# Moving layer-norm statistics, the small product and the running sums of a selective state-space stage to other engines and stages

## The chip, the cores and the metric

The kernel runs on one core of a Trainium2 chip. The metric is the device time of one execution in microseconds (us). The core has a matrix engine (TensorE, PE in the profile; its weight loads are PEld), a vector engine (VectorE, DVE), an engine for activation functions (ScalarE, ACT), a general one (GpSimd, POOL) and one that issues DMAs (SyncE, SP). Each has its own queue of instructions and goes through it in order; they wait for each other by semaphores.

## The reference, cut to what matters

The input x is 32 sequences of 256 tokens of 128 features, with an adjacency matrix of 256x256 for each sequence. Four blocks follow each other, each added to x:

```
x = x + L0_gnn(layernorm(x), adj)      # convolutions, distances, a gated recurrent unit
x = x + L0_ffn(layernorm(x))           # state-space block ("mamba2")
x = x + L1_gnn(layernorm(x), adj)      # d = (sum(adj)+1e-5)**-0.5 ; d*adj*d @ (x @ weight) + bias
x = x + L1_ffn(layernorm(x))           # 8 experts, top 2
```

Of the second block the change touches this:

```
dt    = softplus(layernorm(x) @ W_in[:, 640:644] + dt_bias)     # 4 heads for each token
A     = -exp(A_log)
A_cum = cumsum(dt * A) along the 256 tokens of the sequence (the reference: in chunks of 128)
...     exp(A_cum[l] - A_cum[s]) weighs token s in the output of token l; x*dt enters the sum
out   = Y @ W_out @ W_lin + b_lin
```

## The kernel before, in words

Tokens lie on the 128 partitions: X (x_tokens) holds 64 tiles of 128 tokens by 128 features and stays on the core from stage to stage. A step is 512 tokens (T = 4 tiles, G = 2 sequences), and there are 16 steps. Each stage is a function with a block of its own; between two stages stands a barrier of all engines. There is no planner: the order on each engine is the order in which the code writes it.

The graph stage (gnn_phase) runs a body for each step through every engine, with lags: in VectorE's body number t, part a works on step t-1, b on t-2 and c on t-3, and the last three bodies (16 to 18) only empty the pipeline. Bodies 4 to 15 are a loop with addresses from a register. Part c of a body makes the new state (zd at L455, hT at L458), which TensorE turns back (L566) and VectorE adds to X (L505, semaphore x_updated). Part b ends the body with v (L533) and the argument of n (L537); ScalarE takes its tanh (L430), GpSimd makes x minus tn (L349), and the next body begins with zd. Between zd and the low part of the turned rows (L493) stand the mask product and its split, the normalization of part a (L149), the statistics of the current step (L130, L133), and the sums of the convolution. ScalarE also sums the rows of the adjacency into deg (L438).

The stage of dt (dt_phase) works in 8 pairs of steps. VectorE takes bn_stats (L751) and bn_aggr (L754) of 8 tiles, GpSimd adds epsilon (L708) and takes the power -0.5 (L710), VectorE normalizes (L759), TensorE turns each tile (L798), ScalarE copies the turned rows to XT (L730), and TensorE multiplies each tile with the 4 columns of W_dt (L807): the tile of XT is the stationary operand and 4 columns stream. GpSimd adds the bias b_lin of the block's output to X once a pair is normalized (L716). In the midst VectorE makes dinv from deg (L764 to L768) by one Newton step on ScalarE's exp(-0.5 ln). At the end come, on [128 tokens, 64 tiles x 4 heads], the bias of dt (L775), softplus in three activations (L732 to L736) and a maximum (L778), the product with A (L781), the running sums by two products with a triangle and with ones (L810, L811) and their joining (L783, L785), a transpose (L815), a copy (L742), and two DMAs to DRAM (L692) in the layout of heads by tokens.

The state-space stage (mamba_phase) first reads these sums back, broadcast to all partitions (L866), and runs a software pipeline of 20 bodies. VectorE there adds masks (L952), filters (L968), weighs (L946, L957) and at last updates X (L974) with the output product, four bodies behind the first. GpSimd only takes one power a step (L877). Its weights are loaded by SyncE during the stage of dt (L688). Then follow the dispatch stage and the expert stage.

Of the kernel before, what the change touches and what calls it, by code (L numbers as in the profile page):

```python
# [151 lines left out]
def gnn_phase(nc, x_dram, adjT_dram, adj_dram, w, X, deg, eye):  # L152
# [14 lines left out]
    with ExitStack() as ctx:  # L167
# [26 lines left out]
        rstd = sb("rstd", [P, 2, T])  # L194
        xn = sb("xn", [P, T, P])
# [71 lines left out]
        back_done, x_updated = sem("back_done"), sem("x_updated")  # L267

# [84 lines left out]
        def _(act):  # L353
# [12 lines left out]
            def body(s):  # L366
# [64 lines left out]
                if s.live():  # L431
# [4 lines left out]
                    for j in range(T):  # L436
                        need(act, deg_done, T * s.t + j - 1)
                        act.activation(summed[:, j % 2], adj[:, s.p, j], ACT.Copy, accum_out=deg[:, bass.ds(s.t * T + j, 1)]).then_inc(deg_done, 1)  # L438
# [3 lines left out]
        def _(dve):  # L442
            def body(s):
# [84 lines left out]
                if b.live():  # L528

                    dve.wait_ge(tr_ready, b.t + 1)  # L530
                    dve.wait_ge(gh_ready, b.t + 1)
                    need(dve, u_ready, b.t)
                    dve.scalar_tensor_tensor(out=v[:], in0=tr[:], scalar=1.0, in1=gh[:], op0=ALU.add, op1=ALU.mult).then_inc(rg_ready, 1)  # L533
                    dve.wait_ge(rg_ready, b.t + 1)
                    dve.wait_ge(n_done, b.t + 1)
                    need(dve, tn_ready, b.t)
                    dve.tensor_tensor(n_arg[:], v[:], p_n[:], ALU.add).then_inc(u_ready, 1)  # L537
            run_steps(dve, body, 3)
# [92 lines left out]
def mamba_weights(nc, ctx, w):  # L631
# [7 lines left out]
        "never": ([P, P], w["never"]),  # L639
    }  # L640
# [3 lines left out]
def dt_phase(nc, w, X, XT, table, deg, dinv, next_weights, cum_dram, eye):  # L644
# [3 lines left out]
    PAIR = 2 * T  # L648
    PAIRS = NT // PAIR
    COLS = NT * HEADS  # L650
    with ExitStack() as ctx:
        ph = Phase(nc, ctx, "t_")
        sb, sem = ph.sb, ph.sem
        w_dt = sb("w_dt", [P, HEADS])
        b_lin = sb("b_lin", [P, P])
        dt_bias, A_log, A_neg = (sb(s, [P, HEADS]) for s in ("dt_bias", "A_log", "A_neg"))
        upper, ones = sb("upper", [P, P]), sb("ones", [P, P])
        minus_half = sb("minus_half", [P, PAIR])
        eps = sb("eps", [P, 1])
        stats, mv = sb("stats", [P, 2, PAIR, 6]), sb("mv", [P, 2, PAIR, 2])  # L660
        veps, rstd = sb("veps", [P, 2, PAIR]), sb("rstd", [P, 2, PAIR])
        xn = sb("xn", [P, 2, PAIR, P])
        flat = [P, NT, HEADS]
        u, absu, e, l, dt, dA = (sb(s, flat) for s in ("u", "absu", "e", "l", "dt", "dA"))
        cum, total = sb("cum", flat), sb("total", flat)
        turned = sb("turned", [P, 2, P])
        logs, rough, vr, vrr = (sb(s, [P, NT]) for s in ("logs", "rough", "vr", "vrr"))
        p_xT = [ph.psum(f"p_xT{p}", [P, 2, S]) for p in range(2)]
        p_dt = ph.psum("p_dt", flat)
        p_cum, p_total = ph.psum("p_cum", flat), ph.psum("p_total", flat)  # L670
        p_turned = ph.psum("p_turned", [P, 2, P])
        names = ("loaded next_loaded consts stats_done mv_done veps_done rstd_done xn_ready xT_done XT_ready biased dt_done A_ready "
                 "u_ready e_ready dt_ready dA_ready cum_done cum_ready total_ready turned_done turned_ready table_ready written logs_done rough_done chain")
# [3 lines left out]
        def live(k):  # L677
            return 0 <= k < PAIRS

        @block.sync  # L680
        def _(sp):
            sp.dma_start(b_lin[:], spread(w["b_lin"])).then_inc(q["loaded"], 16)
            sp.dma_start(w_dt[:], w["W_dt"]).then_inc(q["loaded"], 16)
            sp.dma_start(dt_bias[:], spread(w["dt_bias"])).then_inc(q["loaded"], 16)
# [1020 lines left out]
```

## Time and profile before

| | us |
|---|---|
| median of 3 runs | 1245.38 (1243.94 to 1248.22) |
| the profiled execution, own time | 1249.54 |
| its span, first to last instruction | 1247.8 |
| graph stage | 0 to 386.8 |
| stage of dt | 386.8 to 445.5 |
| state-space stage | 445.5 to 766.5 |
| dispatch and expert stages | 766.5 to 1247.8 |

TensorE is busy for 84% of the span, VectorE for 68%, ScalarE for 57%, GpSimd for 32%. Busy time alone does not say what bounds a stage: TensorE's matmuls are pipelined, and its granted clock changes between two levels, 1.0 (2.4 GHz) and 0.5 (1.2 GHz). The mean granted clock over the span is 0.874.

### The profile page before, as it was taken

The page shows a single profiled execution, that of the slowest core. Times are in us where ns is not written, and L with a number is a line of the kernel's source. Part 1 is how long each engine was busy: PE and PEld are TensorE (multiplying, and loading weights), DVE is VectorE, ACT ScalarE, POOL GpSimd, SP SyncE. Part 2 cuts the span into 40 slices and gives each one's busy share as a digit, 9 for nine tenths or more (in the row PEclk, how much of TensorE's full clock was granted, in tenths as well). Part 3 has the DMA queues.
Part 4 walks back from the last instruction along what each step waited for, and adds up shares of the span by engine and source line. Part 5 has one row for each costly group of instructions (what it writes and reads, how often), then busy time and mean ns, then how long its engine had stood idle before and what let it go on. Part 6 is the DMA issues. An engine that isn't in the chain of part 4 may idle for free. (4 is left out here: it accounts for less than half of the span.)

```text
span 1247.8 us, 23207 instructions
## 1 busy us (share of the span) xinstructions
PE 1053.5 (84%) x6746; PEld 925.6 (74%) x6746; DVE 846.9 (68%) x2117; ACT 712.4 (57%) x1560; POOL 400.6 (32%) x413
## 2 busy tenths in 40 slices
PE   2999999999995946899999975567609999899998
PEld 2988889898884924566666665566509999899997
DVE  5576767667667636999999964799854555445554
ACT  4466564655652238888888853666504555455554
POOL 4232232322314600001000001457662444524444
PEclk9999999999996567788788876788658999999999
DMA  4121212112100022123212302735234544333331
GB/s 157 60 69 44 85 42 82 44 44 82 34 1 24 1 72 62 40 68 68 64 47 60 68 1 83 233 112 160 82 128 122 150 127 126 95 96 96 99 95 56
DMA packets 82778, 99.14 MB, mean 79 GB/s; under 512 B 9483, under 2 KB 68626, under 8 KB 82554
## 3 DMA queue, kind: packets, MB, share of 16 engines
q1 hardware_dynamic: 72490, 74.31, 22.0%
q0 software_dynamic: 8752, 21.25, 4.9%
q10 hardware_dynamic: 1440, 2.40, 0.6%
q8 instruction: 48, 0.79, 0.3%
q14 instruction: 48, 0.39, 0.1%
HBM read 72.30 MB, written 27.02 MB: 80 GB/s over the span
## 5 line engine op out<-in xcount | busy, mean ns | idle before, releaser
L1616 PE MATMUL e_p_y<-w,e_gT 128*128 (+1 forms) x852 | 118.2, 275 | 0.0
L1563 DVE TENSOR_TENSOR e_g<-e_sl,e_p_h 128x342 f32<-128x342 f32 x142 | 72.6, 511 | 63.5 <-ACT e_sl L1541 55.5
L877 POOL TENSOR_TENSOR m_rs<-m_ms,m_minus_half 128x4 f32<-128x4 f32 x16 | 18.6, 1164 | 300.5 <-ACT m_ms L910 300.5
L1616 PEld LDWEIGHTS e_p_y<-w,e_gT 128*128 128x128 f32 (+1 forms) x852 | 106.1, 191 | 0.4 <-issue 0.4
L1545 ACT ACTIVATE e_gT<-e_p_gx 128x384 f32<-128x384 f32 x142 | 69.6, 490 | 63.9 <-PE e_p_gx L1606 63.9
L87 PE MATMUL e_p_h<-w_hi,e_xT_hi 128*128 x284 | 104.5, 368 | 1.5 <-DVE e_g L1563 0.8
L1541 ACT ACTIVATE e_sl<-e_p_h 128x342 f32<-128x342 f32 x142 | 64.8, 457 | 69.7 <-PE e_p_h L89 69.5
L1567 DVE TENSOR_TENSOR e_xT_lo<-e_p_gx,e_xT_hi 128x128 fp32r<-128x128 f32 x142 | 41.4, 292 | 86.2 <-ACT e_xT_hi L1549 85.9
L1527 POOL DMA_INDIRECT sorted_scratch<-e_xg x71 | 69.0, 972 | 91.2 <-DVE e_xg L1573 89.6
L1525 POOL DMA_INDIRECT out<-e_xg x71 | 68.9, 970 | 85.9 <-DVE e_xg L1573 79.9
L968 DVE SCALAR_TENSOR_TENSOR m_c<-m_p_x,m_vecs,m_c 128x506 f32<-128x506 f32 (+2 forms) x144 | 95.5, 735 | 0.0
L89 PE MATMUL e_p_h<-w_hi,e_xT_lo 128*128 x284 | 92.1, 324 | 0.0
L88 PE MATMUL e_p_h<-w_lo,e_xT_hi 128*128 x284 | 92.0, 324 | 0.0
L1230 POOL DMA_INDIRECT sorted_scratch<-rows,c_dest x64 | 62.8, 982 | 30.5 <-issue 17.4
L1606 PE MATMUL e_p_gx<-eye,e_g 128*128 128x128 f32 (+1 forms) x426 | 69.6, 272 | 0.0
L1602 PE MATMUL e_p_gx<-eye,e_xg 128*128 128x128 f32 x142 | 39.8, 280 | 30.8 <-DMA e_xg<-sorted_scratch 30.0
L991 PE MATMUL m_p_x<-xT_all,m_w_in 128*128 128x512 f32 x96 | 52.1, 684 | 14.2 <-DVE m_c L968 13.4
L1039 PE MATMUL m_p_zY<-m_W,m_xdt 128*64 128x256 f32 x256 | 61.7, 560 | 2.6 <-DVE m_W L946 2.6
L918 ACT ACTIVATE m_dec<-m_cum,table 128x256 f32<-128x256 f32 x128 | 63.3, 495 | 0.2
L87 PEld LDWEIGHTS e_p_h<-w_hi,e_xT_hi 128*128 128x128 f32 x284 | 55.1, 194 | 2.8 <-issue 2.6
L88 PEld LDWEIGHTS e_p_h<-w_lo,e_xT_hi 128*128 128x128 f32 x284 | 55.2, 194 | 0.0
L89 PEld LDWEIGHTS e_p_h<-w_hi,e_xT_lo 128*128 128x128 f32 x284 | 54.8, 193 | 0.0
(357 smaller groups left out, 3356.3 us busy)
## 6 DMA issues: line engine op xcount, KB each, us to landing
e_xg<-sorted_scratch SPq DMA_DIRECT2D x142, 130.0 KB, 2.1
m_cum<-cum_scratch SPq DMA_DIRECT2D x16, 1024.0 KB
g_adjT<-in_adjT SPq DMA_DIRECT2D x16, 512.0 KB, 4.0
g_adj<-in_adj SPq DMA_DIRECT2D x16, 512.0 KB
c_adjT<-in_adjT SPq DMA_DIRECT2D x16, 512.0 KB, 6.5
x_tokens<-in_x SPq DMA_DIRECT2D x16, 256.0 KB, 5.0
sorted_scratch<-nothing SPq DMA_DIRECT2D x2, 1040.0 KB, 10.1
sorted_scratch<-nothing SPq DMA_DIRECT2D x12, 130.0 KB, 2.6
```

The source lines that it names most:

```text
L87: pe.matmul(out, lhsT.hi, rhs.hi, start=start, stop=False)
L88: pe.matmul(out, lhsT.hi, rhs.lo, start=False, stop=False)
L89: return pe.matmul(out, lhsT.lo, rhs.hi, start=False, stop=stop)
L918: act.activation(dec[:, g, h, lo:hi], rows[b], ACT.Exp, bias=table[:, d * T + 2 * g + b, NEG_CUM, h:h + 1]).then_inc(q["dec_ready"], 1)
L968: dve.scalar_tensor_tensor(out=out, in0=x, scalar=vecs[:, k * TAPS + tap:k * TAPS + tap + 1], in1=out, op0=ALU.mult, op1=ALU.add).then_inc ...
L1525: sent = pool.indirect_dma_start(out_dram, home, xg[:, b, RES:RES + P], None, bounds_check=NT * P - 1, oob_is_err=False)
L1527: sent = pool.indirect_dma_start(sorted_dram[1], home, xg[:, b], None, bounds_check=ROWS - 1, oob_is_err=False)
L1541: act.activation(sl[:, i % 2], p_h1[i % 2][:, 0:HP], ACT.Silu).then_inc(q["sl_ready"], 1)
L1545: act.activation(gT[:, c % D3], p_gx[i % 2][:, 0:len(CH)], ACT.Copy).then_inc(q["gT_ready"], 1)
L1563: dve.tensor_tensor(g[:, i % D3], sl[:, i % 2], p_h3[i % 2][:, 0:HP], ALU.mult).then_inc(q["g_ready"], 1)
L1606: last = pe.transpose(p_gx[i % 2][0:r, k, :], g[:, c % D3, h0:h0 + r], eye[:])
L1616: last = pe.matmul(p_y[d % 2][:, 0:P], gT[0:r, d % D3, k], w2k[:, bass.ts(e, P)], start=k == 0, stop=k == len(CH) - 1)
```

## The change

The change does five things.

1. In the graph stage, VectorE takes the statistics of the updated X (part c of a body): four bn_stats between v and n's argument, four bn_aggr and one copy behind it. Mean and variance go to rows 1 and 2 of a tile `norm` whose row 0 is the old deg.
2. In the stage of dt both roots, of deg and of the variance, are taken at once for all 64 tiles (128 columns): ln and exp on ScalarE, three operations on VectorE. GpSimd's power and the statistics leave the stage, and the 64 normalizations run in a row.
3. The product changes roles: slices of a weight tile that is zero but for W_dt's 4 columns are the stationary operand, 256 columns of XT (a sequence) stream, and 32 such products add up in one bank. Row 4j+h of the result is head h of sequence j. The bias of dt and A are then one number for each row.
4. The running sums are one scan of VectorE along 256 tokens and go to DRAM in one DMA. Two pairs of transposes and four copies of ScalarE bring dt and minus the sums back to the table with tokens on partitions.
5. GpSimd adds b_lin to X in the state-space stage, two adds of 256 columns for each step, behind the power of the step before.

```diff
 # graph stage, VectorE, end of a body
+                    if c.live():
+                        dve.wait_ge(x_updated, c.t + 1)
+                        need(dve, next_norm, c.t)
                     dve.scalar_tensor_tensor(out=v[:], in0=tr[:], ...).then_inc(rg_ready, 1)
+                if c.live():
...
+                    for j in range(T):
+                        dve.bn_stats(next_stats[:, j, :], X[:, c.t * T + j, :]).then_inc(next_stats_done, 1)
+                if b.live():
+                    if c.live():
+                        dve.wait_ge(next_stats_done, T * (c.t + 1))
                     dve.wait_ge(rg_ready, b.t + 1)
...
                     dve.tensor_tensor(n_arg[:], v[:], p_n[:], ALU.add).then_inc(u_ready, 1)
+                if c.live():
...
+                    for j in range(T):
+                        dve.bn_aggr(next_mv[:, j, :], next_stats[:, j, :]).then_inc(next_mv_done, 1)
+                    dve.wait_ge(next_mv_done, T * (c.t + 1))
+                    dve.tensor_copy(norm[:, 1:3, bass.ds(c.t * T, T)], next_mv[:].rearrange("p t k -> p k t")).then_inc(next_norm, 1)
 # stage of dt, SyncE
+            sp.dma_start(per_row[:], w["dt_rows"]).then_inc(q["w_in"], 16)
+            sp.wait_ge(q["cleared"], 1)
+            sp.dma_start(w_dt[:, SEQ_ROWS:P], w["W_dt"]).then_inc(q["w_in"], 16)
...
+            sp.wait_ge(q["cum_ready"], 1)
+            sp.dma_start(cum_dram.rearrange("h (j l) -> j h l", l=N), cum[:]).then_inc(q["written"], 16)
 # stage of dt, GpSimd
+            pool.memset(w_dt[:], 0.0).then_inc(q["cleared"], 1)
 # stage of dt, ScalarE
+            act.activation(logs[:], norm[:, 0:3:2], ACT.Ln, bias=eps[:, 0:1]).then_inc(q["logs_done"], 1)
+            act.activation(rough[:], logs[:], ACT.Exp, scale=-0.5).then_inc(q["rough_done"], 1)
...
+            act.activation(absu[:], p_dt[:], ACT.Abs, bias=per_row[:, 0:1]).then_inc(q["abs_ready"], 1)
+            act.activation(e[:], absu[:], ACT.Exp, scale=-1.0).then_inc(q["e_ready"], 1)
+            act.activation(l[:], e[:], ACT.Ln, bias=1.0).then_inc(q["l_ready"], 1)
+            for k, scale in ((DT, 1.0), (NEG_CUM, -1.0)):
+                act.wait_ge(q["turned_done"], k + 1)
+                for c in range(2):
+                    act.activation(pieces[:, k, c], p_turned[k][:, c]..., ACT.Copy, scale=scale).then_inc(q["table_ready"], 1)
 # stage of dt, VectorE
+            dve.scalar_tensor_tensor(out=vr[:], in0=norm[:, 0:3:2], scalar=EPS, in1=rough[:], ...)   # and two more -> inv
+            for s in range(STEPS):
+                need(dve, q["xT_done"], s - 2)
+                for j in range(T):
+                    t = s * T + j
+                    dve.tensor_scalar(xn[:, s % 3, j, :], X[:, t, :], norm[:, 1, t:t + 1], inv[:, 1, t:t + 1], ALU.subtract, ALU.mult)
+            dve.tensor_scalar(u[:], p_dt[:], per_row[:, 0:1], 0.0, ALU.add, ALU.max)
+            dve.tensor_tensor(dt[:], u[:], l[:], ALU.add)
+            dve.tensor_scalar(dA[:], dt[:], A_pos[:, 0:1], -1.0, ALU.mult, ALU.mult)
+            dve.tensor_tensor_scan(out=cum[:], data0=ones[:], data1=dA[:], initial=0.0, op0=ALU.mult, op1=ALU.add)
 # stage of dt, TensorE: 4 transposes of step s, then the product of step s-1
+                    for g in range(G):
+                        j = b * G + g
+                        last = pe.matmul(p_dt[:], w_dt[:, SEQ_ROWS - HEADS * j:SEQ_ROWS - HEADS * j + P], XT[:, j * N:(j + 1) * N], start=j == 0, stop=j == BS - 1)
 # state-space stage, GpSimd and VectorE
             for s in range(STEPS):
+                for half in range(2):
+                    xt = X[:, s * T + 2 * half:s * T + 2 * half + 2, :]
+                    pool.tensor_tensor(xt, xt, bb, ALU.add).then_inc(q["biased"], 1)
...
                     dve.wait_ge(q["rs_ready"], o + 1)
+                    dve.wait_ge(q["biased"], 2 * (o + 1))
```

The dispatch stage reads row 0 of `inv` in place of dinv, and b_lin is loaded with the weights of the state-space stage.

## Rows read from the trace of the kernel before

**Rows 1.** By stage: stretch, us, busy of PE PEld DVE ACT POOL, clock, DMA.
```profile
0.00:386.80 386.80, 355.76 (x2352) 317.17 (x2352) 256.69 (x519) 214.90 (x441) 113.31 (x131) 0.98 0.20 60
386.80:445.50 58.70, 42.88 (x198) 40.89 (x199) 41.34 (x202) 14.06 (x27) 34.27 (x28) 0.50 0.05 15
445.50:766.50 321.00, 266.10 (x1444) 193.33 (x1444) 262.10 (x336) 237.37 (x434) 18.78 (x19) 0.80 0.23 53
```

**Rows 2.** Timeline of VectorE, one step of the graph stage; start, duration, idle before.
```profile
215.78 0.87 DVE L130 BATCH_NORM_STATS2 g_stats<-x_tokens 128x6 f32 x4
216.56 0.37 DVE L133 BATCH_NORM_AGGREGATE g_mv<-g_stats 128x2 f32<-128x6 f32 x4
...
219.99 0.69 DVE L493 TENSOR_TENSOR g_xs_lo<-g_p_xT,g_xs_hi 128x512 fp32r<-128x512 f32 x1 [0.28 <-ACT g_xf L379]
...
228.62 0.69 DVE L533 SCALAR_TENSOR_TENSOR g_v<-g_tr,g_gh 128x512 f32<-128x512 f32 x1 [1.41 <-ACT g_tr L424]
229.35 0.69 DVE L537 TENSOR_TENSOR g_n_arg<-g_v,g_p_n 128x512 f32<-128x512 f32 x1
232.20 0.69 DVE L455 SCALAR_TENSOR_TENSOR g_zd<-g_tz,g_xd 128x512 f32<-128x512 f32 x1 [2.17 <-POOL g_xd L349]
```

**Rows 3.** Groups of the graph stage, 85 to 350 us; busy, mean ns, idle before.
```profile
L493 DVE TENSOR_TENSOR g_xs_lo<-g_p_xT,g_xs_hi 128x512 fp32r<-128x512 f32 x12 | 8.3, 692 | 4.5 <-ACT g_xf L379 4.5
...
L87 PE MATMUL g_p_nmp<-g_xs_hi,g_w_lr_hi 128*64 128x512 f32 x12 | 5.0, 416 | 1.7 <-DVE g_xs_lo L493 1.4
```

**Rows 4.** Timeline of the start of the stage of dt.
```profile
386.77 1.28 ACT L720 ACT_TABLE_LOAD   x1 [5.90 <-PEq L101]
...
388.44 0.26 ACT L724 ACTIVATE t_rough<-t_logs 128x64 f32<-128x64 f32 x1
...
391.20 2.14 DVE L759 TENSOR_SCALAR t_xn<-x_tokens,t_mv,t_rstd 128x128 f32<-128x128 f32 x8
...
392.37 2.14 PE L798 MATMUL t_p_xT<-eye,t_xn 128*128 128x128 f32 x8 [7.55 <-DVE t_xn L759]
```

**Rows 5.** Groups of the stage of dt, 391 to 435.1 us.
```profile
L807 PEld LDWEIGHTS t_p_dt<-t_w_dt,xT_all 128*128 128x128 f32 x128 | 29.1, 333 | 0.1
...
L759 DVE TENSOR_SCALAR t_xn<-x_tokens,t_mv,t_rstd 128x128 f32<-128x128 f32 x64 | 20.0, 382 | 0.3 <-POOL t_rstd L710 0.2
L716 POOL TENSOR_TENSOR x_tokens<-x_tokens,t_b_lin 128x1024 f32<-128x1024 f32 x8 | 18.8, 2353 | 2.3 <-DVE t_xn L759 2.3
```

**Rows 6.** Timeline of the stage of dt in its steady part.
```profile
404.40 1.83 PEld L807 LDWEIGHTS t_p_dt<-t_w_dt,xT_all 128*128 128x128 f32 x8
...
405.97 0.90 PEld L798 LDWEIGHTS t_p_xT<-eye,t_xn 128*128 128x128 f32 x4
```

**Rows 7.** Timeline of the end of the stage of dt.
```profile
435.06 0.42 DVE L775 TENSOR_TENSOR t_u<-t_p_dt,t_dt_bias 128x256 f32<-128x256 f32 x1 [8.67 <-PE t_p_dt L807]
...
441.81 1.25 SPq L692 DMA_DIRECT2D cum_scratch<-t_turned  x2
```

**Rows 8.** Busy time and granted clock (third number from the end) of short stretches.
```profile
447.50:451.70 4.20, 4.20 (x5) 1.84 (x6) 0.00 (x0) 1.17 (x2) 0.00 (x0) 0.50 0.68 136
451.70:455.10 3.40, 2.43 (x6) 0.76 (x4) 0.15 (x1) 2.09 (x3) 0.00 (x0) 1.00 0.89 278
...
810.10:813.50 3.40, 3.40 (x25) 3.22 (x24) 1.34 (x4) 2.71 (x9) 3.40 (x1) 1.00 0.55 154
```

**Rows 9.** Timeline of TensorE in the dispatch stage, ahead of 810.1.
```profile
806.00 3.62 PE L1425 MATMUL c_p_agg<-c_adjT,c_xs 128*128 128x256 f32 x8
809.41 0.95 PE L1431 MATMUL c_p_xT<-eye,rows 128*128 128x128 f32 x4
```

**Rows 10.** Groups of later stages; for L1319 durations, ns min/median/max.
```profile
L974 DVE SCALAR_TENSOR_TENSOR x_tokens<-m_p_o,m_rs,x_tokens 128x128 f32<-128x128 f32 x64 | 17.8, 339 | 11.0 <-POOL m_rs L877 11.0
...
L1360 DVE TENSOR_TENSOR_SCAN c_upto<-c_restart,c_hot 128x144 f32<-128x144 f32 x8 | 3.7, 461 | 0.3
...
L1319 DVE SCALAR_TENSOR_TENSOR c_vr<-c_mv,c_rough x19: 129/158/4800, 769.2 to 895.5; 128x8 f32<-128x8 f32 x19
```

More of the change, by code:

```diff
@@ L672, in dt_phase @@
-        names = ("loaded next_loaded consts stats_done mv_done veps_done rstd_done xn_ready xT_done XT_ready biased dt_done A_ready "
-                 "u_ready e_ready dt_ready dA_ready cum_done cum_ready total_ready turned_done turned_ready table_ready written logs_done rough_done chain")
+        w_dt = sb("w_dt", [P, SEQ_ROWS + P])
+        per_row = sb("per_row", [P, 2])
+        A_pos = sb("A_pos", [P, 1])
+        eps = sb("eps", [P, 1])
+        ones = sb("ones", [P, N])
+        both = [P, 2, NT]
@@ L781, in _ @@
[L781 to L787 removed]
+            dve.wait_ge(q["A_ready"], 1)
@@ L810, in _ @@
-            pe.matmul(p_cum[:], upper[:], dA[:], start=True, stop=True).then_inc(q["cum_done"], 1)
-            pe.matmul(p_total[:], ones[:], dA[:], start=True, stop=True).then_inc(q["cum_done"], 1)
-            pe.wait_ge(q["cum_ready"], 2)
-            for c in range(2):
-                half = cum[:, c * (NT // 2):(c + 1) * (NT // 2)].rearrange("p t h -> p (t h)")
-                last = pe.transpose(p_turned[:, c], half, eye[:])
-            last.then_inc(q["turned_done"], 1)
+                    for g in range(G):
+                        j = b * G + g
+                        last = pe.matmul(p_dt[:], w_dt[:, SEQ_ROWS - HEADS * j:SEQ_ROWS - HEADS * j + P], XT[:, j * N:(j + 1) * N], start=j == 0, stop=j == BS - 1)
@@ L819, in mamba_phase @@
+            last.then_inc(q["dt_done"], 1)
+            for k, (src, ready) in enumerate(((dt, "dt_ready"), (cum, "cum_ready"))):
+                pe.wait_ge(q[ready], 1)
+                for c in range(2):
+                    last = pe.transpose(p_turned[k][:, c], src[:, c * P:(c + 1) * P], eye[:])
+                last.then_inc(q["turned_done"], 1)
 def mamba_phase(nc, weights, X, XT, table, cum_dram, eye):
@@ L829, in mamba_phase @@
         sb, sem = ph.sb, ph.sem
-        w_in, w_outT, w_lin, vecs, D, never = (weights[name][0] for name in ("w_in", "w_outT", "w_lin", "vecs", "D", "never"))
+        w_in, w_outT, w_lin, vecs, D, never, b_lin = (weights[name][0] for name in ("w_in", "w_outT", "w_lin", "vecs", "D", "never", "b_lin"))
         w_out = sb("w_out", [P, 2, P])
```

197 lines of the change are left out of this document (66 added, 131 removed).

## The prediction

> **What bounds the kernel now.** I read the stages first, by stretches [rows 1]: the graph stage up to 386.8 us, the stage of dt from there to 445.5 (58.7 us), the state-space stage to 766.5. The engines separate what bounds each. In the graph stage TensorE is busy for 355.8 of 386.8 us at a granted clock of 0.98, and what can lengthen it is whatever makes TensorE wait. In the stage of dt TensorE's matmul row is busy for 42.9 of 58.7 us at 0.50, the lower of its levels (1.2 GHz), with VectorE at 41.3 beside it. Next the groups of that stage [rows 5] and its order of time [rows 6]: once it runs, TensorE alternates 8 weight loads of the product (1.83 us, so 0.23 each, two passes for each tile of tokens) with 4 transposes (0.90), 2.46 us from one step to the next. The product streams 4 columns and pays 128 rows of weights for them. The rest of the stage is a start (392.4 before TensorE begins) and a chain of single operations at the end, from 435.06 to 445.5 [rows 1, 7].
>
> The graph stage I read by one step of VectorE [rows 2], because the change puts work between two of its lines. A step is 22 us. After n's argument (229.35) VectorE idles 2.17 us until GpSimd has x minus tn, then runs with hardly a gap to the low part of the transposed rows (219.99), before which it idles 0.28. Over 12 steps that idle time is 4.5 us, 0.37 a step, and TensorE's first product on these rows waited 1.4 us in all for that very line [rows 3]. So TensorE's order and the loop through VectorE are nearly equally long.
>
> **The change part by part.** All against the profiled execution (span 1247.8, own time 1249.54), which lies 4.2 us above the median 1245.38; differences are carried over unscaled.
>
> (1) *Statistics in the graph stage.* Per step VectorE gets 4 bn_stats between v and n_arg, and 4 bn_aggr and a small copy behind n_arg. The same forms take 0.87 and 0.37 there [rows 2]; the copy of 8 elements is not shown in that stage, I bound it by 0.1 and 0.4 and take 0.2. The aggregation and copy (0.6) lie in the 2.17 idle behind n_arg. The statistics do not lie beside anything: n_arg starts 0.04 behind v's end now, in the changed kernel 0.91 later. Queued behind n_arg are ScalarE's tanh, GpSimd's subtraction, VectorE's zd, and then VectorE's unbroken row of work down to the low part at 219.99. Its idle 0.37 absorbs a part; 0.91-0.37 = 0.54 us reach TensorE. It is a loop from step to step, so it is paid each time: the statistics stand in bodies 3 to 15, the low part behind each in bodies 4 to 16, 13 times: +7.0 us. Ends: 0 (TensorE has slack I don't see), and 13x1.28 = 16.6 (aggregation on the path too and no idle time). In the last two bodies VectorE has no statistics and normalization of its own left, which covers it; only behind the last update of X nothing covers: 0.87+0.37+0.2 = +1.4 us ahead of the barrier. Sum of (1): +8.4.
>
> (2) *Start of the stage of dt.* Gone: statistics and GpSimd's power; now in series: table load 1.28 and two activations [rows 4], 128 wide instead of 64 (the second took 0.26; I take 0.4 and 0.3), three VectorE operations of 128 columns at 0.29 (between the 0.26 of that row and the 0.42 of the 256 wide one in rows 7), then 4 normalizations of 0.27 (8 in 2.14). With the gaps TensorE starts some 4.2 us into the stage instead of 5.6 (392.37). GpSimd now clears the weight tile before SyncE may load the 4 columns of W_dt, and ScalarE's 16 copies and TensorE's first product stand behind that load. It is issued some 0.5 us in, and the first product wants it at about 5.5; the nearest row, the write of the sums, has 3.7 us from issue to the next stage with two issues in it [rows 1, 7], so it lands in time. If that cover is gone, its lateness (up to 1 us) is paid once.
>
> (3) *The product.* 32 products of 256 columns, each two passes, in place of 64x2 weight-bound ones: 4 passes a step. Nearest row: 128x256 f32 passes, 8 in 3.62 us at the low level, so 0.43 each (the last one's latency off), 0.21 by half at the high one [rows 9]. The loads hide under 256 columns there. With 4 transposes (0.90 low [rows 6], 0.45 high) a step is 4x0.43+0.90 = 2.62 us low and 1.31 high. At the low level nothing is gained over 2.46. The level decides. In the trace it rose behind products streamed back to back in the next stage, low at 447.5 and high at 451.7 [rows 8]; at 810.1 it was high after 256-column products at the low level and 4 transposes [rows 8, 9]. It stayed low through 43 us of 4-column products and transposes. The new mixture has long products in each step with transposes between, nearer to 806-810 than to the old stage. I take: low for the first two steps (5.2 us), then high: 14x1.31 = 18.3. VectorE, no longer with statistics, needs 64x0.27 = 17.3 us, under TensorE's 23.5; at the old stage's mean of 0.38 it would be 24.3, about TensorE's time. That mean has GpSimd's 8 adds of 2.35 us beside it [rows 5], and those leave. Product until the last result: 5.2+18.3+0.3 = 23.8, ends 21.0 (high at once) and 42.3 (never).
>
> (4) *End of the stage.* Three activations of 256 (0.45 with their gaps), sum 0.45, times A 0.4, scan. The scan's nearest row is 144 wide in 0.46 [rows 10]; by length 0.8, ends 0.42 (the elementwise row of rows 7) and 0.85. Then one write to DRAM instead of two; from its issue at 441.81 to the next stage are 3.7 us [rows 1, 7], of which 1.25 were two issues; one goes: 3.1. Transposes and table copies (about 1.3 us behind the scan) lie beside the write. 1.35+0.45+0.4+0.8+3.1 = 6.1 us against 10.4.
>
> Stage: 4.2+23.8+6.1 = 34.1 against 58.7: -24.6.
>
> (5) *Bias in the next stage.* 32 adds of 256, by 2.35 for 1024 some 0.6 us, 18.8 in all, on GpSimd, which is busy for 18.8 of 321 us there [rows 1]. Two stand behind each power; VectorE at that time works on taps and on forms with one operand in PSUM. In the stage behind, where GpSimd adds rows too, those forms never stretched (339 ns mean over 64 [rows 10] for the update of X), while an 8-wide one with both inputs in SBUF went from a median of 158 ns to 4800 at most [rows 10]. I take 0; ends 0 and +18.8 (every add blocks VectorE). It gives nothing back, since it is added work. The new wait on the bias stands four steps behind the adds. The stage's running sums still come by the same DMA behind the same barrier.
>
> **Sum**: +8.4-24.6+0 = -16.2: 1249.5 becomes 1233.3, the median 1245.4 becomes 1229.2.
>
> **Rivals.** (A) the forecast, 1229: chance 0.50. (B) The statistics in the graph stage find cover, as the busy TensorE there suggests (0.98 clock, almost no gaps): no +7.0, so 1222. For it: most of TensorE's products waited for nothing; against: rows 3. Chance 0.17. (C) TensorE's clock stays at 1.2 GHz, because the transposes between the products break the activity. Stage 4.2+42.3+6.1 = 52.6, -6.1; with +8.4 that is +2.3: 1247.7, and up to 1253 when the aggregation (13x0.37) stands on the path as well. It decides from where the stage is longer than 50.3 us (58.7-8.4), there it is slower than before. For: the old stage never rose with transposes in it; against: 810.1. Chance 0.20. The Trainium skill, "TensorE: Matmul & The Clock Gate", section "PE-mode transpose", says that transposes don't count as busy time for the clock in the same way; by that rule this rival gains, and no row here separates them. (D) The adds in the state-space stage hold up VectorE, which is busy 262 of 321 us: half of the 18.8 gives 1239. Against: 339 ns. Chance 0.08. Small rest 0.05, spread over the ends.
>
> **Numbers.** 0.3% (3.7 us) is what can be told from no change. Faster by more: A, B, D and a little of the rest, 0.75. Within: C mostly, 0.13. Slower by more: C's upper part, 0.12. Range: B's 1222 less 2 for a clock that rises at once, to C's 1247: 1220 to 1247.
>
> **What would show it.** In the profile after: bn_stats between v and n_arg, the idle time before the low part gone, and TensorE's first product on it waiting about 0.5 us in each step (B: no wait); granted clock of the new stage mostly 1.00 (C: 0.50) and a step of 1.3 us (C: 2.6); from the last product to the next stage 6 us; two-input SBUF lines of the state-space stage unstretched (D: stretched). The prediction is wrong if the stage of dt takes over 45 us or the graph stage grows by less than 3 or more than 14 us.

## The result and the profile after

| us | before | changed |
|---|---|---|
| median, same chip | 1244.8 (1243.66 to 1248.22, 5 runs) | 1223.17 (1221.25 to 1223.77, 5 runs) |
| ratio to before | | 0.9818, interval 0.9801 to 0.9834 |
| profiled execution, own time | 1249.54 | 1222.53 |
| graph stage | 386.8 | 389.2 |
| stage of dt | 58.7 | 34.4 |
| state-space stage | 321.3 | 315.2 |
| dispatch, expert stage | 166.2, 314.8 | 166.4, 315.4 |

The changed kernel is 21.6 us faster by the medians; 16.2 were forecast. Its 1223.2 lies nearer to rival B (1222) than to the forecast (1229); what that is worth is said behind the experiments. Stages below are cut at the table load that opens each, which puts the state-space stage of the kernel before at 321.3 us.

Stretches of the changed kernel (busy of PE, PEld, DVE, ACT, POOL; granted clock third from the end). The first three rows answer to [rows 1], the last two cut the stage of dt where the clock rose:

```profile
0.00:389.20 389.20, 354.90 (x2352) 316.05 (x2352) 272.37 (x663) 215.16 (x440) 113.53 (x130) 0.99 0.20 59
389.20:423.60 34.40, 25.24 (x132) 20.77 (x132) 20.32 (x71) 13.95 (x27) 0.59 (x3) 0.80 0.09 24
423.60:738.80 315.20, 262.00 (x1444) 190.66 (x1444) 262.03 (x336) 236.96 (x434) 40.44 (x51) 0.81 0.24 54
389.20:398.80 9.60, 5.27 (x18) 4.28 (x19) 6.53 (x25) 3.83 (x7) 0.59 (x3) 0.50 0.27 70
398.80:419.30 20.50, 18.59 (x111) 15.91 (x110) 12.71 (x45) 9.23 (x17) 0.00 (x0) 1.00 0.01 1
```

VectorE's busy time moved with the statistics: +15.7 us in the graph stage, -21.0 in the stage of dt. The stage lost 24.3 us: its clock went from 0.50 throughout to 1.00 for 20.5 us of it, and its two ends got shorter.

The steady part of the stage of dt, changed kernel, timeline (start, duration); it answers to [rows 6]:

```profile
400.65 0.60 PE L772 MATMUL t_p_xT<-eye,t_xn 128*128 128x128 f32 x4
400.98 0.73 PEld L780 LDWEIGHTS t_p_dt<-xT_all,t_w_dt 128*128 128x128 f32 x4
401.08 1.03 PE L780 MATMUL t_p_dt<-xT_all,t_w_dt 128*128 128x256 f32 x4
401.29 1.12 DVE L751 TENSOR_SCALAR t_xn<-x_tokens,norm,inv 128x128 f32<-128x128 f32 x4 [0.19 <-PE t_p_xT L772]
401.95 0.60 PE L772 MATMUL t_p_xT<-eye,t_xn 128*128 128x128 f32 x4
```

From one group of four transposes to the next are 1.30 us. VectorE waits for TensorE (0.19), not the reverse. Its end, answering to [rows 7]:

```profile
415.41 1.98 PE L780 MATMUL t_p_dt<-xT_all,t_w_dt 128*128 128x256 f32 x8
...
417.43 0.47 ACT L726 ACTIVATE t_absu<-t_p_dt,t_per_row 128x256 f32<-128x256 f32 x1 [1.22 <-PE t_p_dt L780]
...
418.90 0.42 DVE L756 TENSOR_TENSOR t_dt<-t_u,t_l 128x256 f32<-128x256 f32 x1 [0.48 <-ACT t_l L730]
419.36 0.35 DVE L759 TENSOR_SCALAR t_dA<-t_dt,t_A_pos 128x256 f32<-128x256 f32 x1
...
419.75 0.69 DVE L762 TENSOR_TENSOR_SCAN t_cum<-t_ones,t_dA 128x256 f32<-128x256 f32 x1
...
420.47 0.61 SPq L703 DMA_DIRECT2D cum_scratch<-t_cum  x1
```

The second pair of turned pieces is copied by 421.7, and the next stage begins at 423.6: the write sets the end, as forecast.

VectorE in one step of the graph stage, changed kernel, answering to [rows 2] (figures in brackets: idle time):

```profile
207.07 0.69 DVE L538 SCALAR_TENSOR_TENSOR g_v<-g_tr,g_gh 128x512 f32<-128x512 f32 x1 [1.41 <-ACT g_tr L426]
207.68 0.87 DVE L544 BATCH_NORM_STATS2 g_next_stats<-x_tokens 128x6 f32 x4
208.58 0.69 DVE L551 TENSOR_TENSOR g_n_arg<-g_v,g_p_n 128x512 f32<-128x512 f32 x1
209.18 0.38 DVE L556 BATCH_NORM_AGGREGATE g_next_mv<-g_next_stats 128x2 f32<-128x6 f32 x4
209.71 0.17 DVE L558 COPY norm<-g_next_mv 128x8 f32 x1
211.42 0.69 DVE L457 SCALAR_TENSOR_TENSOR g_zd<-g_tz,g_xd 128x512 f32<-128x512 f32 x1 [1.54 <-POOL g_xd L351]
...
219.66 0.48 DVE L488 SCALAR_TENSOR_TENSOR g_v<-g_odd,g_scales,g_xf 128x256 f32<-128x256 f32 x1
220.05 0.69 DVE L491 TENSOR_TENSOR g_nm_lo<-g_p_nmp,g_nm_hi 128x512 fp32r<-128x512 f32 x1
220.65 0.68 DVE L495 TENSOR_TENSOR g_xs_lo<-g_p_xT,g_xs_hi 128x512 fp32r<-128x512 f32 x1
```

The idle time ahead of the low part (L495) is gone. How little that cost is read below.

### The profile page after: what moved, and what is told of

Its sections match the earlier page's. It is cut to its first block and busy times, and to the rows that moved or that the text cites. A ratio compares the mean times of both kernels' runs of the same rounds, so it can differ in the third digit from the quotient of the medians.

```text
span 1220.7 us, 23165 instructions
## 1 busy us (share of the span) xinstructions
PE 1028.3 (84%) x6680; PEld 898.8 (74%) x6680; DVE 842.0 (69%) x2130; ACT 712.4 (58%) x1561; POOL 388.8 (32%) x421
## 5 line engine op out<-in xcount | busy, mean ns | idle before, releaser
L942 DVE SCALAR_TENSOR_TENSOR m_c<-m_p_x,m_vecs,m_c 128x506 f32<-128x506 f32 (+2 forms) x144 | 95.6, 740 | 0.0
```

What stands on the lines that cost most here:

```text
L942: dve.scalar_tensor_tensor(out=out, in0=x, scalar=vecs[:, k * TAPS + tap:k * TAPS + tap + 1], in1=out, op0=ALU.mult, op1=ALU.add).then_inc ...
```

## The experiments

The runs lie on several chips. On two of them (one had the first set of four, the other the statistics taken twice) the dispatch stage takes 177 to 180 us and not 166, and before itself has a median of 1259, so ratios and the other stages are compared. The first set: again, statistics back, statistics behind, warm start.

**Again.** The changed kernel, unchanged, on another chip, to compare the others of its set with.

> The changed kernel again, as a control for its neighbours and for how much a stage's length differs from one execution to another. Theory 1 (the state-space stage is 5.8 us shorter for a reason in the change): that stage takes 315 to 316 us again, total 1223. Rival (it was that execution's fall of the clock's rises and of the reads of the running sums): that stage comes out anywhere from 315 to 321 us.

Ratio 0.9819 (0.9786 to 0.9853); graph 389.8, dt 34.8, state-space 314.8 us. It reproduces, stage by stage.

**Statistics back in the stage of dt**, in a row ahead of the roots; the graph stage as before.

```diff
-                if c.live(): ... dve.bn_stats(next_stats[:, j, :], X[...]) ... dve.bn_aggr(...) ... dve.tensor_copy(norm[:, 1:3, ...])
+            for t in range(NT):
+                dve.bn_stats(stats[:, t, :], X[:, t, :]).then_inc(q["stats_done"], 1)
+            for t in range(NT):
+                dve.wait_ge(q["stats_done"], t + 1)
+                dve.bn_aggr(mv[:, t, :], stats[:, t, :]).then_inc(q["mv_done"], 1)
```

> Undoes part 1 alone: 64 bn_stats (0.20 us each, back to back) and 64 bn_aggr (0.08) and one copy stand at the start of the stage of dt on VectorE, the graph stage has none. Theory 1 (in the graph stage the statistics cost next to nothing, 0.11 us a step and 1.4 at the end): the graph stage is 2.4 us shorter, 386.8 again, the stage of dt longer by 13.2+5.0+0.2-1 (the table load runs beside) = 17.5, total 1223.2-2.4+17.5 = 1238. Rival (they cost 0.54 us a step there, and something else in that stage was quicker in the profiled execution): the graph stage is 8.4 us shorter, total 1232.

Ratio 0.9916 (0.9889 to 0.9943). Graph 386.9, so the moved statistics cost that stage 3.0 us (389.82 against 386.85); dt 50.5, so they would cost 15.7 there (17.5 expected). Of their 16.8 us little more than the table load beside them is covered in a stage of dt built like this one: its groups there (busy, mean ns, idle before) are

```profile
L722 DVE BATCH_NORM_STATS2 t_stats<-x_tokens 128x6 f32<-128x128 f32 x64 | 12.5, 288 | 1.3 <-PEq L101 1.3
L725 DVE BATCH_NORM_AGGREGATE t_mv<-t_stats 128x2 f32<-128x6 f32 x64 | 4.3, 175 | 0.0
```

**Statistics behind n's argument**, so that tanh and all behind it start no later.

```diff
-                    for j in range(T):
-                        dve.bn_stats(next_stats[:, j, :], ...)          # between v and n_arg
                     dve.tensor_tensor(n_arg[:], v[:], p_n[:], ALU.add).then_inc(u_ready, 1)
                 if c.live():
+                    for j in range(T):
+                        dve.bn_stats(next_stats[:, j, :], ...)
                     for j in range(T):
                         dve.bn_aggr(next_mv[:, j, :], ...)
```

> Moves the four bn_stats of the graph stage from before n's argument to behind it, ahead of the aggregation; the aggregations then wait one by one. Theory 1 (VectorE's idle 1.54 us before zd takes them in, and what they cost before n's argument is the 0.11 us a step): 13x0.11 = 1.4 us faster than the changed kernel, 1221.8; the graph stage ends 1.4 us sooner. Rival A (the step's length comes from TensorE alone and the 0.11 is the waits and addresses): no difference. Rival B (0.87+0.37+0.17 plus the gaps do not fit before x minus tn arrives: 2.17 us before): up to 0.3 us a step slower, 1227.

Ratio 0.9812 (0.9784 to 0.9841), graph 387.4: 0.5 us above the kernel without statistics there. One step of it, timeline:

```profile
228.70 0.69 DVE L543 TENSOR_TENSOR g_n_arg<-g_v,g_p_n 128x512 f32<-128x512 f32 x1
229.30 0.86 DVE L549 BATCH_NORM_STATS2 g_next_stats<-x_tokens 128x6 f32 x4
230.09 0.37 DVE L552 BATCH_NORM_AGGREGATE g_next_mv<-g_next_stats 128x2 f32<-128x6 f32 x4
230.60 0.94 DVE L554 COPY norm<-g_next_mv 128x8 f32 x1
231.55 0.69 DVE L457 SCALAR_TENSOR_TENSOR g_zd<-g_tz,g_xd 128x512 f32<-128x512 f32 x1
```

n's argument starts 0.73 us behind v again, and the whole set fits in the time that VectorE waits for GpSimd. The gain of 2.4 us in that stage (389.8 to 387.4, where 1.4 was expected) is seen in the profile; the medians of the total, 1237.4 and 1237.5, show no gain.

**Statistics taken twice**, the second set between v and n's argument too, into a spare tile.

```diff
+                    for j in range(T):
+                        dve.bn_stats(spare[:, j, :], X[:, c.t * T + j, :])
                     for j in range(T):
                         dve.bn_stats(next_stats[:, j, :], X[:, c.t * T + j, :]).then_inc(next_stats_done, 1)
```

> The changed kernel with each step's four statistics between v and n's argument taken twice; the second set goes to a tile that nobody reads (about +0.8 us of VectorE per step, 13 steps). The first set cost the graph stage about 1.5 us in its loop where 7.0 was forecast. Theory A (the loop had 0.7 us of slack per step, and the first set used it up): now every further us is paid, 13 x 0.8 = +10 us, graph stage 398 to 401 instead of 389.5, VectorE's zd starts every 22.8 to 22.9 us instead of 22.11, no idle time ahead of the low part of the turned rows, total about 1233. Theory R (TensorE has a large reserve there and statistics at this place cost little whatever their number): graph stage +1 to +3 us (390 to 392.5), total about 1225.

Graph 401.1, +11.3 on the 389.8 of the changed kernel's second profile (+11.9 on the first): 13 x 0.8 = 10.4, and 0.8 more behind the last update of X, which the expectation left out. zd starts every 22.92 us (103.73 to 332.96 in 10 steps) against 22.11 and, in the kernel before, 22.00. What TensorE's first product on the low part waited for it, 12 steps of the changed kernel, then of this one (groups; last column the wait):

```profile
L87 PE MATMUL g_p_nmp<-g_xs_hi,g_w_lr_hi 128*64 128x512 f32 x12 | 5.1, 421 | 3.1 <-DVE g_xs_lo L495 3.1
```

```profile
L87 PE MATMUL g_p_nmp<-g_xs_hi,g_w_lr_hi 128*64 128x512 f32 x12 | 5.0, 418 | 12.9 <-DVE g_xs_lo L496 12.9
```

1.4 before [rows 3], 3.1, 12.9: the first set of 0.8 us a step adds 0.14 to that wait, the second 0.82. Theory A holds: there was slack, the first set used it up, and from there each microsecond is paid. The total, 1247.81 (ratio 0.9908, 0.9887 to 0.993), lies above both forecasts, which were written for a chip with a dispatch stage of 166 us; it took 179.8. By the ratios the second set costs 0.0090 (0.9818 to 0.9908), 11.3 us of 1259.

**The old roles in the product**: the tile of X^T stationary, 4 columns streamed, everything else as changed; its output is another.

```diff
-                        last = pe.matmul(p_dt[:], w_dt[:, SEQ_ROWS - HEADS * j:...], XT[:, j * N:(j + 1) * N], start=j == 0, stop=j == BS - 1)
+                        last = pe.matmul(p_dt[:, t * HEADS:(t + 1) * HEADS], XT[:, t * P:(t + 1) * P], w_dt[:, SEQ_ROWS:P], start=True, stop=True)
```

> Undoes the roles of the product alone: each tile of XT is the stationary operand again and the 4 columns of W_dt stream, 64 products of two passes; everything behind it is as in the changed kernel and so works on numbers in another layout (the output is another). Theory 1 (the stage is short because the streamed products let TensorE's clock rise): the granted clock stays at 0.50 through the stage, a step takes 8x0.23+0.90 = 2.46 to 2.7 us again, the product 39 to 43 us instead of 23.4, the whole stage 50 to 54 instead of 34.4. Rival (VectorE's freed time is what made it short, and the clock only followed a TensorE without gaps): the clock rises here too, 8x0.12+0.45 = 1.4 us a step, stage 35 to 37 us.

Ratio 0.9953 (0.9933 to 0.9973). Its stage of dt:

```profile
389.17:439.47 50.30, 41.16 (x196) 39.84 (x196) 20.30 (x71) 13.95 (x27) 0.59 (x4) 0.50 0.06 16
```

50.3 us at a clock of 0.50, at the lower end of theory 1. The rest of the change is worth 58.7 - 50.3 = 8.4 us in this stage, the roles of the product 15.9. It also shows that in the old stage's steady part the statistics and GpSimd's adds hid behind TensorE: without them its step is still 2.46 us (groups of transposes at 401.96, 404.42, 406.87).

**Half the columns** in all products but the first: 128, as wide as a transpose.

```diff
+                        n = N if j == 0 else P
+                        last = pe.matmul(p_dt[:, 0:n], w_dt[:, ...], XT[:, j * N:j * N + n], start=j == 0, stop=j == BS - 1)
```

> 31 of the 32 products stream 128 of the 256 columns; the rest of the sum is left out. The transposes are the same, so more of TensorE's time goes to transposes than to products. Theory 1 (transposes let the clock rise too, products need not be most of the work): the clock rises as in the changed kernel within 10 us of the first transpose, and the step is bound by VectorE's normalizations, 1.1 to 1.2 us: product part 21 us, stage 31 to 33. Rival (transposes do not count, the streamed products alone raise it, as the Trainium skill says of transposes in TensorE: Matmul & The Clock Gate, section PE-mode transpose): with half the streaming the clock stays at 0.50, a step takes 4x0.23+0.90 = 1.8 us, product part 29 us, stage 40 us.

Ratio 0.9772 (0.9737 to 0.9806), dt 28.9 us, under the 31 to 33 expected. Its clock in stretches of 2 us:

```profile
396.00:398.00 2.00, 2.00 (x10) 1.86 (x9) 1.64 (x7) 0.37 (x2) 0.00 (x0) 0.50 0.00 0
398.00:400.00 2.00, 2.00 (x15) 2.00 (x15) 1.61 (x6) 1.10 (x2) 0.00 (x0) 0.72 0.00 0
400.00:402.00 2.00, 2.00 (x20) 1.92 (x18) 2.00 (x9) 1.29 (x3) 0.00 (x0) 1.00 0.02 4
```

It rises 5.5 us behind the first transposes, 5.3 in the changed kernel, although half of what TensorE streams now are transposes. So rival C's reason, that transposes between the products keep the clock low, doesn't hold for this kernel's f32 transposes; with the same transposes and 4-column products between them it stays low. Whether the transposes helped it up, or the products alone were enough, this run doesn't show.

**A warm start**: two 512-column products on X, whose results nobody reads, ahead of the first transposes.

```diff
+            for i in range(2):
+                pe.matmul(p_xT[3][:], eye[:], X[:, i * T:(i + 1) * T, :].rearrange("p t d -> p (t d)"), start=True, stop=True)
```

> Two products of 512 columns of X with the identity, their result unused, at the start of the stage of dt, where TensorE waits for the first normalized tiles. They take 4x0.85 = 3.4 us at the low clock, from 389.6 to 393.1, and TensorE's own work starts at 393.5. Theory 1 (the level rises behind products streamed back to back): it rises up to 3.4 us sooner, so 1 to 2 of the steps at 2.6 us take 1.3: 0.5 to 2.5 us faster than the changed kernel, 1221 to 1222.5. Rival (the level rises only once the real products run, or the extra products delay the first transposes): 0 to 0.5 us slower.

Ratio 0.9806 (0.9777 to 0.9834); dt 32.2 against 34.8. The clock rose some 3 us into the stage, ahead of the first transposes (394.30):

```profile
390.00:392.00 2.00, 1.96 (x3) 0.96 (x4) 0.00 (x0) 1.96 (x3) 0.59 (x3) 0.50 0.11 7
392.00:394.00 2.00, 1.62 (x3) 0.21 (x1) 1.75 (x7) 0.24 (x2) 0.00 (x0) 0.67 0.81 257
394.00:396.00 2.00, 1.34 (x9) 1.10 (x10) 2.00 (x9) 0.60 (x1) 0.00 (x0) 1.00 0.30 65
```

Its gain is 2.6 us against its neighbour, 2.1 against the first profile of the changed kernel. More than that can't be read from it, because the length of the low part varies by itself: from the first transposes to the rise are 5.3 us in the changed kernel, 6.2 in its second profile, 3.6 with the statistics behind, and between 4.6 and 6.3 in the five other profiles that begin the stage in the same way. The medians of the total, 1235.8 and 1237.5, lie 1.7 us apart.

**The bias back in the stage of dt**, 8 adds of 1024 on GpSimd beside the 64 normalizations.

```diff
+            for k in range(STEPS // 2):
+                pool.wait_ge(q["xn_ready"], 2 * T * (k + 1))
+                xt = X[:, 2 * T * k:2 * T * (k + 1), :]
+                pool.tensor_tensor(xt, xt, bb, ALU.add)
-                    (the two adds for each step of the state-space stage)
```

> Undoes part 5 alone: GpSimd adds the bias in the stage of dt again, 8 adds of 128x1024 (2.35 us each) behind the normalizations of two steps, none in the state-space stage. Theory 1 (a normalization cannot run beside a GpSimd operation that reads SBUF: it waits for its whole length): VectorE gets 64x0.27+8x2.35 = 36 us of work in a stretch of 23, so the stage is 8 to 13 us longer, 43 to 47. Rival A (only part of it meets, as in the kernel before, where the group's mean was 0.38): 64x0.38 = 24.3 us, the stage 1 to 3 us longer. Rival B: TensorE bounds the stretch and hides it all: 0. The state-space stage stays at 315 us if the adds cost nothing there.

Ratio 0.99 (0.9874 to 0.9926); dt 43.4, the state-space stage 315.8. The normalizations, in the changed kernel and in this one (groups of the stage):

```profile
L751 DVE TENSOR_SCALAR t_xn<-x_tokens,norm,inv 128x128 f32<-128x128 f32 x64 | 17.5, 342 | 3.0 <-PE t_p_xT L772 3.0
```

```profile
L757 DVE TENSOR_SCALAR t_xn<-x_tokens,norm,inv 128x128 f32<-128x128 f32 x64 | 31.3, 566 | 0.0
L717 POOL TENSOR_TENSOR x_tokens<-x_tokens,m_b_lin 128x1024 f32<-128x1024 f32 x8 | 19.6, 2449 | 16.7 <-DVE t_xn L757 10.6 <-DMA m_b_lin<-in_b_lin 6.0
```

Eight normalizations take 4.16 us from one add's start to the next (398.86, 403.02, 407.19), where 8 in the changed kernel take 2.24 of work: each add holds VectorE for some 1.9 of its 2.46 us. The durations of the 64 (ns, min/median/max) show how: most are not stretched, and the longest is as long as an add.

```profile
L757 DVE TENSOR_SCALAR t_xn<-x_tokens,norm,inv x64: 332/335/2450, 392.5 to 423.4; 128x128 f32<-128x128 f32 x64
```

The stage takes 9.0 us more (43.4 for 34.4): theory 1, at its lower end.

**No bias adds**: b_lin is not added at all.

```diff
-                for half in range(2):
-                    xt = X[:, s * T + 2 * half:s * T + 2 * half + 2, :]
-                    pool.tensor_tensor(xt, xt, bb, ALU.add).then_inc(q["biased"], 1)
```

> The bias is left out altogether (the output lacks it): no adds in the state-space stage, no wait for them. Theory 1 (the adds cost nothing there): total and the length of that stage as in the changed kernel, 315 +-1.5. Rival (they hold up VectorE's operations with two inputs in SBUF now and then): the stage is 3 to 10 us shorter. It also tells whether the 5.8 us by which that stage is shorter than before has to do with the adds: then it is 321 here.

Ratio 0.9811 (0.9783 to 0.9839). State-space stage 315.6 us with no adds, 315.2 with them. VectorE's largest group of that stage and the adds, changed kernel, then the same group without adds:

```profile
L942 DVE SCALAR_TENSOR_TENSOR m_c<-m_p_x,m_vecs,m_c 128x506 f32<-128x506 f32 (+2 forms) x144 | 95.6, 740 | 0.0
L848 POOL TENSOR_TENSOR x_tokens<-x_tokens,m_b_lin 128x256 f32<-128x256 f32 x32 | 22.6, 728 | 0.1
```

```profile
L938 DVE SCALAR_TENSOR_TENSOR m_c<-m_p_x,m_vecs,m_c 128x506 f32<-128x506 f32 (+2 forms) x144 | 95.5, 735 | 0.0
```

The 22.6 us of adds cost nothing that the stage shows. Where they lie says why, and how far that goes. From the second to the thirteenth pair of adds they stand beside L931 and L942, which read PSUM (one pair at 566.70 to 568.11, L931 at 566.24, L942 from 567.38), the last three beside L920 and L949, which do too. The forms with both inputs in SBUF (L913, 1224 ns against 1225; L926, 1224 and 1220 against 1221 and 1217) are not stretched because the adds miss them, but for one overlap of 0.28 us. The kernel before shows in its stage of dt what such a form, of 64 columns, can cost: a neighbour of the same form took 0.21 us.

```profile
397.80 2.35 POOL L716 TENSOR_TENSOR x_tokens<-x_tokens,t_b_lin 128x1024 f32<-128x1024 f32 x1
397.88 2.34 DVE L766 SCALAR_TENSOR_TENSOR t_vrr<-t_vr,t_rough 128x64 f32<-128x64 f32 x1
```

**Before, a second profile.** The state-space stage was 4.3 to 6.8 us shorter in all nine profiles taken by then of the changed kernel and its variants than in the first profile of before, and nothing in the forecast said so.

> The kernel before, unchanged, for a second profile. Question: the state-space stage, which the change hardly touches, was 321.3 us long in the first profile of before and 314.6 to 316.9 in every changed kernel. Theory V (variation: the first profile of before belongs to an execution 4.2 us above its median, and the excess lies in this stage): this profile has the stage at 315 to 317.5 us, the first running sums about 7.8 us after the stage's start (9.48 then), and a step of 17.06 us (17.40 then). Theory S (systematic: the layout of the write, the address of the sums in DRAM or the addresses of the tiles on the core differ between the kernels): stage again at 320 to 322 us, 9.4 to 9.5 us, 17.4 us. The other stages in both: graph 386.8, dt 58.7, dispatch 166 or 180 (by chip), experts 315.

**Two writes** of the running sums, in halves.

```diff
-            sp.dma_start(cum_dram.rearrange("h (j l) -> j h l", l=N), cum[:]).then_inc(q["written"], 16)
+            halves = cum_dram.rearrange("h (j c l) -> c j h l", c=2, l=P)
+            for c in range(2):
+                sp.dma_start(halves[c], cum[:, c * P:(c + 1) * P]).then_inc(q["written"], 16)
```

> The changed kernel with its running sums written to DRAM in two DMAs of 128-token halves (rows of 512 bytes), as the kernel before did, in place of one with rows of 1 KB. Theory L (the layout and number of the writes makes the readback slow): the stage of dt grows by 0.6 us (one more issue), the first running sums come 9.4 us after the start of the state-space stage instead of 7.8, and that stage grows by 2 us or more; total 2 to 6 us above the changed kernel. Theory V (variation): stage of dt +0.6 (34.4 to about 35.0), first sums at 7.7 to 7.9 us, state-space stage 315 to 317, total +0.6 us.

The second profile of before has graph 385.9, dt 58.7, state-space 316.9 us, own time 1244.17: 4.5 us of the difference (321.34 to 316.85) were not the change. Its first sums came after 8.6 us, between the two forecasts. With two writes the first sums came after 7.7 us, so the layout of the write doesn't delay them; yet this profile has a state-space stage of 320.2 (ratio 0.9825, 0.9788 to 0.9863). Both long profiles have one step of the pipeline, a different one, that is long (start to start of GpSimd's power: 19.8 us in before, 19.5 in the one with two writes; elsewhere 16.7 to 17.7 in the steady part). The clock goes with it. The kernel before, first profile, around its long step, then the second profile at the same step:

```profile
591.50:593.50 2.00, 0.00 (x0) 0.00 (x0) 2.00 (x3) 1.99 (x6) 1.26 (x1) 0.54 0.00 0
...
599.50:601.50 2.00, 2.00 (x17) 1.59 (x15) 1.58 (x5) 1.89 (x3) 0.00 (x0) 0.50 0.66 188
601.50:603.50 2.00, 2.00 (x11) 1.08 (x8) 1.18 (x2) 0.85 (x3) 0.00 (x0) 0.90 0.86 169
```

```profile
589.50:591.50 2.00, 0.05 (x1) 0.05 (x1) 2.00 (x3) 1.99 (x6) 0.49 (x1) 0.54 0.00 0
...
595.50:597.50 2.00, 2.00 (x22) 1.68 (x20) 2.00 (x5) 1.98 (x3) 0.00 (x0) 0.75 0.19 65
597.50:599.50 2.00, 2.00 (x13) 1.13 (x11) 2.00 (x6) 1.99 (x3) 0.00 (x0) 1.00 0.59 178
```

In each step of that stage the clock falls to 0.50, here some 0.2 us after TensorE's work ends ahead of a wait (591.4 in the first profile, 589.4 in the second). In the second profile it is low from 589.7 to 596.5, in the first from 591.7 to 601.9 (the mixed slices read as shares of both levels): 6.8 and 10.2 us, and the step is 2.1 us longer (19.8 for 17.7). The next step has 6.8 for 3.4 us at the low level and is 0.9 us longer (17.7 for 16.8). Of the other 1.5 us, 1.1 lie ahead of the first power (the first sums came 0.9 later) and 0.4 elsewhere. Summed over the stage, the low level holds for 130 us in the first profile of before and 129 in the one with two writes (321.3 and 320.2 us long), and for 117 to 122 in seven other profiles (314.6 to 317.0 us). What decides in an execution when it comes back, I can't tell from these traces. The first sums' time (9.5, 8.6 before; 7.7 to 8.5 in all changed ones) may hold a further difference of a microsecond that stays open; two profiles of before are few.

**Both**: statistics behind n's argument and the warm start together.

> Candidate better than both: the changed kernel with its statistics behind n's argument in the graph stage (alone: graph stage -2.4 us, stage of dt -1.3) and two 512-column products of TensorE on X at the start of the stage of dt, whose results nobody reads, ahead of the first transposes (alone: stage of dt -2.6). Theory F (the terms add): graph stage 387.4, stage of dt 31 us, total 5 us below the changed kernel, ratio to before about 0.978. Theory G (given back later: in each of the two kernels alone the state-space stage was about 2 us longer, 317 against 314.8): state-space stage 317 us, total 2.5 to 3 us below the changed kernel, ratio about 0.980.

1219.07 us (1218.26 to 1220.81), ratio 0.9787 (0.9759 to 0.9814): the lowest time of a kernel that does the whole work. Graph 387.0, dt 32.2, state-space 315.2. The graph's gain is there in full. Of the two gains in the stage of dt (1.3 and 2.6 alone) the sum shows only one: in the profile with the statistics behind n's argument the clock had risen 2.6 us earlier than in its neighbour (3.6 us behind the first transposes, not 6.2), and the warm start leaves nothing of that to win. Nothing was given back in the state-space stage, so theory G falls by the stages and theory F holds but for that overlap; the ratio, 0.9787 between their 0.978 and 0.980, doesn't decide. Against the changed kernel's 0.9818 the intervals overlap, so that it is better rests on the stages.

## Why the prediction was right, and where it wasn't

**Stage of dt: right, step by step.** TensorE started 4.3 us into it (4.2 forecast), the product took 23.9 from 393.53 to 417.39 (23.8), the end 6.2 (6.1); 34.4 for 34.1. The clock was low for the first 5.3 us of TensorE's work (5.2 taken) and the high step 1.30 (1.31 from [rows 6, 9]). That the 5.2 was met so closely is luck: in eight profiles that begin the stage in this way the low part was 3.6 to 6.3 us. The bounds beside 23.8 are some tenths off by the prediction's own terms: 16x1.31+0.3 = 21.3, not 21.0, and 16x2.62+0.3 = 42.2, not 42.3. The scan of 256 took 0.69, within 0.42 to 0.85. The load of W_dt was in time: the first product waited for no DMA. That the product's form was what kept the old stage's clock low is shown by the kernel with the old roles. The gain of the 16 steps lies in the clock: at the low level a new step takes 2.66 us (its products begin at 395.46 and 398.12), more than the old 2.46. The gain of the stage without the roles, 8.4, is more than the 5.7 of the forecast's start and end: the 16 steps also lost the stalls that the old pairs had (42.7 us from the first transposes to the bias of dt [rows 4, 7], which at 2.46 a step would be 39.4).

**Rival C** needed the clock to stay low. It rose with transposes between products of 256 columns, and with products as narrow as the transposes. The Trainium skill's sentence that transposes don't count as busy time in the same way ("TensorE: Matmul & The Clock Gate", "PE-mode transpose") gave it weight. The granted 1.00 of the half-column rows shows that as much of this kernel's transposes as of products did not hold the clock down; whether they count is open, since the products alone may have been enough.

**Graph stage: the term that was mis-sized, and rival B.** "0.91-0.37 = 0.54 us reach TensorE", 13 times, +7.0. Measured: 0.11 us a step (22.00 to 22.11), 1.4 in all, with the tail 1.5 (1.4 forecast); 3.0 (2.97) between the two kernels of one set, 2.4 and 3.3 against the two profiles of before. The prediction had set 3 us as the least growth with which it would hold: of the three, one is clearly under it, one on it, one above. Rival B (no +7.0, so 1222) had this term nearly right, and 1223.2 is its number; not all of it, since TensorE's wait did grow (1.4 to 3.1 us) and the cover ends at once behind the first set. The forecast's total was 5.4 us off, and its range held. Both parts of the 0.54 were wrong in the same direction:
- What is added. I took four bn_stats as 0.87, their busy time. n's argument starts 1.51 behind v and not 0.73, so it is put off by 0.78: the first bn_stats starts 0.08 before v's recorded end (207.68, 207.76).
- What absorbs it. Of the step before, from the timeline of [rows 2]:

```profile
218.46 0.49 DVE L486 SCALAR_TENSOR_TENSOR g_v<-g_odd,g_scales,g_xf 128x256 f32<-128x256 f32 x1
219.01 0.69 DVE L489 TENSOR_TENSOR g_nm_lo<-g_p_nmp,g_nm_hi 128x512 fp32r<-128x512 f32 x1
```

zd starts 4.35 behind v instead of 3.58 (+0.77), but the low part starts 9.23 behind zd (220.65, 211.42) instead of 9.78 (219.99, 210.21; -0.55). Idle time says 0.28 of this. The rest is between starts: 0.98 from the mask product's low part (219.01) to L493 before, 0.60 after (220.05 to 220.65), which is 0.28 of idle time and 0.10 of lost overlap; and 0.55 against 0.39 ahead of that one (218.46 to 219.01, 219.66 to 220.05), a wait of 0.16 that was too short to be listed as idle. The steps alternate, and in every second one there is more: the low part starts 9.84 behind zd before and 9.08 after (-0.76). There the 0.77 is absorbed whole and the next v comes 22.02 us behind the last; in the others 0.2 us are left and it comes 22.21 behind. The mean of the two is the 22.11.

That it is slack, and ends, is shown by the statistics taken twice; that its place is behind n's argument, by the stage's length in the kernel that moves them (the total doesn't show it).

**Bias adds: right**, rival D falls: 315.2 with, 315.6 without. The reason given (forms with a PSUM operand) fits: 740 against 735 ns, and the adds lie beside such forms. What they would cost beside L913 or L926 no run shows; L766 before, 2.34 us beside an add, says that it would not be nothing. The other half of the step, that their leaving the stage of dt is what keeps VectorE under TensorE, was worth 9.0 us there, more than I had said: a mean of 566 for 342 ns, where the prediction took 380. The Trainium skill ("SBUF — State Buffer", "Who interferes with whom") describes a pair of ports that VectorE and GpSimd hold exclusively for a whole instruction, which `tensor_scalar` can need and a form with at most one SBUF input outside the fast modes doesn't; the longest normalization, 2450 ns beside adds of 2449, agrees, and so does the state-space stage.

**State-space stage: not foreseen, and mostly not the change.** 4.5 of the 6.1 us are the difference between two executions of the kernel before; 3.0 of them stand in two steps with more time at the low clock. The 1.6 that are left are of the size of the spread among the changed kernels (314.6 to 317.0 without the two writes), so they can't be put down to the change. Against the second profile of before (1244.17, near the median 1244.8) the sum closes: graph +3.3, dt -24.3, state-space -1.6, the rest +0.9, together -21.7, measured -21.6. Of the 5.4 us between this and the forecast, 5.1 are the graph stage.

## What to carry to other kernels

Read slack by starts, not by idle time: compare start-to-start distances along the engine's row, and if it matters put the same work in twice; the first copy may be nearly free where the second costs its full length. A forecast whose total comes out can still have a term wrong: here +8.4 was 3. A small product with few output columns belongs on the side of the weights, as zero-padded stationary slices with the long dimension streaming: that let TensorE's clock rise, from which all of the gain per step came (2.46 to 1.30 us; 2.66 while the clock was low). A term read from one profile of a stage whose clock goes up and down needs a second profile before a few microseconds of it are believed.

## Of the hardware, not expected

- The same state-space stage took 316.9 and 321.3 us in two executions of one kernel, with 130 us at the low clock in the longer one and 122 in the other.
- GpSimd's adds of X cost VectorE's one-input normalizations 14 us of busy time in 31.3 (566 for 342 ns), nearly all of it in a few that last as long as an add (median 335, longest 2450 ns; seven such make up 14.8 us), and its filter products in the state-space stage 5 ns in 740.
- A copy of 8 elements behind the statistics took 0.17 us, and 0.94 (230.60 to 231.54) where GpSimd's subtraction ran beside it (230.22 to 231.51).
- The clock rose 3.6 to 6.3 us behind TensorE's first transposes in eight profiles of the same start of a stage.
